# Wide attention's round: value products and projections behind the first two transposes, both key products behind the third

## What is computed

```python
xn = _layernorm(x, ln1_w, ln1_b)          # x here is the context, 77 tokens
latn = _layernorm(latents, ln2_w, ln2_b)  # the 128 tokens of the sequence
q = latn @ Wq
kv = concatenate([xn, latn], axis=1) @ Wkv
k, v = split(kv, 2, axis=-1)              # 205 keys, 16 heads of 64
weight = softmax(einsum('bhld,bhnd->bhln', q * scale, k * scale))
out = einsum('bhln,bhnd->bhld', weight, v).reshape(b, l, 1024)
return out @ Wo
```

## Time and profile before

| | us |
|---|---|
| median of 3 runs | 2099.02 |
| lowest and highest | 2098.89, 2105.73 |
| profiled execution | 2097.34 |
| its span | 2095.6 |

### The profile page before, as it was taken

The page is one execution under the profiler, slowest core; times in us unless marked ns, Lnnn a source line. Parts: engine busy times, 40 slices in busy tenths (PEclk is TensorE's granted clock), DMA queues, the critical chain, the costliest instruction groups (busy, mean ns, idle before and its releaser), DMA issues.

```text
span 2095.6 us, 45982 instructions
## 1 busy us (share of the span) xinstructions
PE 1925.5 (92%) x15235; PEld 1543.7 (74%) x15297; DVE 1463.9 (70%) x3292; ACT 1345.6 (64%) x3094; POOL 970.4 (46%) x1173
## 2 busy tenths in 40 slices
PE   6999999999999999974089999999899999999998
PEld 4877778888888888842078888887677777777776
DVE  5668667777666666657865676767787788677775
ACT  4676567777677677757745666787555555555554
POOL 3555543344344344300026555554366566556565
PEclk8999999999999999997589999999999999999999
DMA  6533300000000000000033434555233333333332
GB/s 182 170 116 110 94 2 2 2 2 2 2 2 2 2 2 2 2 1 1 0 99 99 120 103 109 155 165 160 69 117 122 122 121 124 114 119 122 121 128 91
DMA packets 139168, 161.12 MB, mean 77 GB/s; under 512 B 15340, under 2 KB 99244, under 8 KB 138796
## 3 DMA queue, kind: packets, MB, share of 16 engines
q1 hardware_dynamic: 132780, 153.46, 24.1%
q10 hardware_dynamic: 6160, 4.78, 0.7%
HBM read 119.75 MB, written 38.70 MB: 76 GB/s over the span
## 4 chain that ended last, share of the span: by engine, by line
PE 69%; issue 8%; POOL 8%; DVE 5%; ACT 5%; SPq 2%; DMA 2%; POOLq 0%; ACTq 0%; DVEq 0%
POOL h_lo L2245 7%; PE bank L993 6%; PE score_banks L273 6%; PE bank L1009 6%; PE score_banks L982 5%; PE bank L934 5%; PE bank L935 4%; PE bank L936 4%; PE bank L284 3%; PE score_banks L255 3%; PE score_banks L1902 3%; PE score_banks L1900 3%; PE score_banks L1901 3%; PE bank L1900 2%; PE score_banks L254 2%
## 5 line engine op out<-in xcount | busy, mean ns | idle before, releaser
L2245 POOL TENSOR_TENSOR h_lo<-h,h_hi 128x512 fp32r<-128x512 f32 x264 | 341.1, 1292 | 245.1 <-ACT h_hi L2026 245.0
L1432 POOL TENSOR_TENSOR pw<-ew,rw 128x410 f32<-128x410 f32 x256 | 222.5, 869 | 369.2 <-DVE rw L1282 369.2
L556 DVE TENSOR_REDUCE nmx<-score_banks 128x4 fp32r<-128x512 f32 (+1 forms) x384 | 237.4, 620 | 182.6 <-PE score_banks L255 179.3
L2019 ACT ACTIVATE sl<-score_banks 128x512 f32<-128x512 f32 x264 | 157.8, 598 | 240.1 <-PE score_banks L1902 237.6
L449 ACT ACTIVATE pt<-score_banks 128x512 f32<-128x512 f32 (+1 forms) x384 | 229.4, 599 | 119.8 <-PE score_banks L273 118.9
L2164 DVE TENSOR_TENSOR bank<-score_banks,sl 128x512 f32<-128x512 f32 x264 | 184.1, 697 | 144.2 <-PE score_banks L1902 114.3
L1146 ACT ACTIVATE ew<-score_banks,nmax 128x205 f32<-128x205 f32 x512 | 217.5, 434 | 103.1 <-DVE nmax L1275 101.9
L708 POOL TENSOR_SCALAR_AFFINE_SELECT pt<-pt 128x512 f32<-128x512 f32 x256 | 164.6, 643 | 177.2 <-ACT pt L449 177.2
L273 PE MATMUL score_banks<-q_pack,k_diag 128*128 128x128 f32 (+1 forms) x1536 | 236.8, 278 | 0.1
L273 PEld LDWEIGHTS score_banks<-q_pack,k_diag 128*128 128x128 f32 (+1 forms) x1536 | 188.4, 179 | 45.2 <-issue 36.4
L1900 PE MATMUL score_banks<-x_hi,w_hi 128*128 128x512 f32 x528 | 209.7, 397 | 0.1
(11 more groups left out here) (348 smaller groups left out, 4572.5 us busy)
## 6 DMA issues: line engine op xcount, KB each, us to landing
share_b<-share_rows SPq DMA_DIRECT2D x256, 256.0 KB, 3.1
q_rows<-q_hi SPq DMA_DIRECT2D x96, 128.0 KB, 2.8
q_pack<-q_rows SPq DMA_DIRECT2D x32, 384.0 KB
raw<-in_experts SPq DMA_DIRECT2D x33, 192.0 KB, 3.3
q_rows<-q_lo SPq DMA_DIRECT2D x48, 128.0 KB, 2.7
k_diag<-k_rows SPq DMA_DIRECT2D x64, 96.0 KB
q_pack<-q_rows SPq DMA_DIRECT2D x31, 192.0 KB
k_diag<-k_rows SPq DMA_DIRECT2D x124, 48.0 KB
```

What stands on the lines that cost most here:

```text
L556: nc.vector.tensor_reduce(m.nmx[:, b % 2, :, 0, c], m.score[c % 2][:, 0:HC * a.columns].rearrange("p (h k) -> p h k", h=HC)[:, :, 0:a.keys ...
L1432: nc.gpsimd.tensor_tensor(m.pw[:, n, :, :], m.ew[:, n % 2, :, :], m.rw[:, n % 2, :].unsqueeze(2).broadcast_to([128, 2, KW]), ALU.mult)\
L2245: nc.gpsimd.tensor_tensor(m.h_lo[:, k % 3, :], m.h[:, (k + u) % 2, :], m.h_hi[:, k % 3, :].bitcast(F32), ALU.subtract).then_inc(s.los, 1)
```

## The change

On TensorE the same operations are put in another order. Before, a round went: queries, value, T0, value, T1, half projection, key 2i+4, T2, key 2i+5, half projection, T3. Now it goes: queries, T0, value, half projection, T1, value, half projection, T2, key 2i+5, key 2i+4, T3. On VectorE the two value copies move behind one maximum each: the first copy now stands between maxima 2 and 3, the reciprocal of step 0 and maximum 2 come ahead of it. The semaphore `keyed`, which counted key products in order, becomes two, since the order of the two changes.

```diff
@@ class WideSemaphores
-        self.keyed = sem(f"{stage}_keyed")
+        self.first_keyed = sem(f"{stage}_first_keyed")
+        self.second_keyed = sem(f"{stage}_second_keyed")
@@ wide_tensor, key
-                 m.kvt_hi[:, v, :, 0:KP], m.kvt_lo[:, v, :, 0:KP]).then_inc(s.keyed, 1)
+                 m.kvt_hi[:, v, :, 0:KP], m.kvt_lo[:, v, :, 0:KP])\
+            .then_inc((s.first_keyed, s.second_keyed)[couple % 2], 1)
@@ wide_tensor, body
             queries(i + 2, m.mix)
+        transpose_probs(i, 0)
+        if ahead:
             pe.wait_ge(s.first_keys, i + 2)
...
             value(tile, m.ask)
-        transpose_probs(i, 0)
+        if i > 0:
+            project_out(i - 1, 0)
+        transpose_probs(i, 1)
         if ahead:
             pe.wait_ge(s.queries, i + 3)
             value(tile + 1, m.mix)
-        transpose_probs(i, 1)
         if i > 0:
-            project_out(i - 1, 0)
-        if ahead:
-            pe.wait_ge(s.values, tile + 1)
-            key(2 * i + 4, m.ask)
+            project_out(i - 1, 1)
         transpose_probs(i, 2)
         if ahead:
             pe.wait_ge(s.values, tile + 2)
             key(2 * i + 5, m.mix)
-        if i > 0:
-            project_out(i - 1, 1)
+            key(2 * i + 4, m.ask)
         transpose_probs(i, 3)
@@ wide_scalar, copy_keys
-        act.wait_ge(s.keyed, couple + 1)
+        act.wait_ge((s.first_keyed, s.second_keyed)[e], i + 1)
@@ wide_vector, copy_keys
-        dve.wait_ge(s.keyed, couple + 1)
+        dve.wait_ge(s.first_keyed, i + 1)
@@ wide_vector, body
             copy_queries(i + 2, m.mix)
-            copy_values(tile, m.ask)
         if ahead:
             reciprocals(i + 1, 0)
             maxima(i + 1, 2)
+        if more:
+            copy_values(tile, m.ask)
+        if ahead:
             maxima(i + 1, 3)
         if more:
             copy_values(tile + 1, m.mix)
```

More of the change, by code:

```diff
@@ L1129, in input_highs @@
         wait(act, s.valued, TILES * (p - 1))
-        wait(act, s.keyed, XC * (p - 1))
+        wait(act, s.first_keyed, QUADS * (p - 1))
+        wait(act, s.second_keyed, QUADS * (p - 1))
         wait(act, s.asked, QUADS * (p - 1))
```

## The result

| | before | after |
|---|---|---|
| median of the runs | 2102.38 us | 2123.0 us |
| lowest and highest | 2098.89, 2105.85 | 2118.34, 2129.04 |
| profiled execution | 2097.34 us | 2118.34 us |
| its span | 2095.6 us | 2116.6 us |
| first scores of the stage to the last | 624.2 us | 640.4 us |

The ratio is 1.0092, with a 95% interval of 1.0062 to 1.0121: slower by some 19 us, 13 to 25. The forecast was 2134.5, 35.5 more than before, in a range of 2112 to 2147. The sign and the mechanism held; the size was 1.8 times too large.

What follows compares the result with a forecast made beforehand. TensorE's order and its bank hand-overs were taken to bound each round. Longer rounds 15.5, the keys' copy 17.7 and VectorE's lateness 2.3 sum to 35.5 us: 2097.34 becomes 2132.8, plus 1.7 for the median, 2134.5; range 2112 to 2147.

Steps and rivals of the forecast that it cites:

- a round starts on VectorE's word: Round start on TensorE: the queries' weights load when VectorE has finished us_lo, plus 0.18 for the signal.
- Step 1: Behind T0, 0.70 earlier: ScalarE's copy waits for step 0's exponentials, starts at 586.09 instead of 586.47, gaining 0.38.
- the bound that I had priced at 6 us less: ScalarE's copy behind T0 may start 0.1 before the accumulator read ends; T1 comes 0.1 earlier, total 2128.
- Step 2: Ahead of T1 on TensorE: a stall of 0.18 for the bank's copy stays where 0.23 was.
- Steps 3 and 4: From T1 to behind T2: T2 is free, then the key product into mix waits for the second value copy, 0.33.
- The hidden-copy rival: Behind T2: the key product finds its bank free, T3 comes 0.07 earlier than before; +14, 2113 us; 10%.
- Step 5: Keys then T3, at 590.26 instead of 590.00: a round 0.25 longer, 15.5 us over 62 rounds.
- The first keys' copy: Behind T3, rounds g = 0 and 1: input or output transposes wait for bank ask, 0.59 in 30 rounds, 17.7 us.
- VectorE's lateness: Norm-step rounds of the first six pairs: keys' copy 1.42 later exceeds the slack to us_lo, 2.3 us over six rounds.
- no signal at all at 16 us less: Waits on VectorE: if its signal cost nothing, 0.18 less in 92 waits, total 2118.
- The faster one: Whole round: only hand-overs bound it, gaining 0.26, 2083 us, if T0's, value and first keys' copies come early enough; 3%.
- weights that are loaded ahead: TensorE's queue: by the skill's rule weights would be in the array before a stall ends, the sum some 9 lower.

Runs made afterwards that it cites:

- e2: The changed kernel with its two key products swapped (2i+4 into ask first) in rounds g = 0 and 1 alone; stage 622.2 us against 640.4.
- e6: The kernel before with the two waits of each transpose group swapped, the bank's first; stage 617.2 us against 624.2, ratio 0.9967.
- e5: The kernel before without TensorE's waits that an earlier wait covers, from the third round on; stage 623.5 us against 624.2, ratio 1.0032.

## Why the prediction was right, and where it was off

*No instruction is added or removed; the bound is the order.* Right: 45982 instructions before and after. But *a round starts on VectorE's word* was wrong: `us_lo` starts two rounds, not all, and from this the 0.18 was read.

*Step 1, the copy behind T0 is held by the exponentials.* Right in kind. T0 came 0.69 earlier (0.70 said). The copy starts 1.68 behind the queries' weights where I had 1.76: at 581.47, while the last accumulator read runs from 581.38 to 581.58. I had let it start only as that read ends. This is the bound that I had priced at 6 us less.

*Step 2, T1 still stalls.* 0.10, where 0.18 was said; the difference is the 0.08 of step 1.

*Steps 3 and 4, a new stall behind T2 for `vs`.* Right, in each of 62 rounds; 0.2 in size, not 0.33. The copy starts where I put it, the moment its product is there. The term that failed is the signal: 0.18 in the sum, 0.05 in the run. The hidden-copy rival (2113) is out by the 13.5 us of this wait on record.

*Step 5, a round is 0.25 longer.* It is 0.03. Key product and T3 add up as said (1.24 against 1.21); T3 stands 5.75 behind the queries' weights, where I had 5.93. A further 0.05 comes from what I hadn't costed: T3 no longer waits for the bank, its weights are loaded 0.19 ahead of its matmul, and the weighting starts 0.53 behind T3 instead of 0.58. Of 15.5 us, 1.6 were real.

*The first keys' copy, 0.59 in 30 rounds.* Right in place and count, 0.48 each in size (0.50 and 0.52 more a round, less the 0.03 of every round), so 14.4 for 17.7. Again it is the 0.13 of the signal. A slip of 0.02 went the other way: by the sum's own rows the weights were free to load at +0.36 (0.39 less 0.03), not at +0.38, so 0.61 less 0.13 is the 0.48. e2 shows the place of the two key products as the cause: with key 2i+4 first in those rounds alone, the stage loses 18.1 us, more than the whole change had added.

*VectorE's lateness, 2.3 us.* It didn't come at all: the rounds in question take 9.76 to 9.79 like their neighbours, and `us_lo` ends 0.16 to 0.17 ahead of the queries' weights as everywhere, or 0.05 in the round that was late before as well. From the start of the keys' copy to `us_lo` those rounds had 4.43 us (5.34 in the late one), and have 1.46 less, as the later copy demands. Idle time gave a part of that. The rest is that VectorE's work became shorter: the records of the norm steps sum to 0.8 to 1.4 us less in each of the twelve rounds (last section). The two late rounds didn't get later by it: the queries' weights came 2.54 and 2.37 behind the first scores before, 2.50 and 2.40 after.

By terms: 35.5, less 13.9 for the round, 3.3 for the keys' wait and 2.3 for VectorE, is 16.0; the stage shows 16.1. The 35.5 was too large mainly because one misread number, 0.13 too large, stood in 92 waits: 12.0 of the 19.5. Step 1's 0.08 in 62 rounds is 5.0 more, and VectorE 2.3; what is left is small and of both signs. The bound that I gave for it, no signal at all at 16 us less, was the right place to look, and I chose the middle without asking whether `us_lo` really released those weights. Another round, the late one at 434.88, would have told. The total, 2123.0, lies in the range but 1 us below the 2124 to 2147 that were the forecast's own part of it.

*Rivals.* The faster one named three conditions, and none came true: the copy behind T0 started too late, the value copy still takes 0.69, the keys' copy 0.58. As for weights that are loaded ahead, T3's in the changed kernel have nothing to wait for and load 0.19 ahead of their matmul, while in every waiting row shown here the weights load 0.05 to 0.11 behind the release (0.22 in e2). The Trainium skill says that weight loads are pulled ahead of matmuls in flight (TensorE: Matmul & The Clock Gate, "Step-by-step: what each phase is for"); the trace agrees for T3, and no weights were pulled ahead of a wait.

## What to carry to other kernels

Count a reordering by each shared bank: product, copy, next user. Work that is moved to cover one copy uncovers another, and here the copy that was uncovered stood in 30 of 64 rounds, in a branch of the code that the change doesn't touch. Before you price a hand-over from one gap, find a round in which the same release comes really late: only then does the gap measure the signal. And where several waits stand ahead of an instruction, write first the one that is released last; here that alone took 7 us off.

## What I hadn't expected of the hardware

**Which wait rides on the instruction.** Of the waits written ahead of a weight load, the trace has the first on the load itself and the further ones in semaphore instructions ahead of it on TensorE's queue, one or two waits in each, 0.05 long: the one for the bank stands at 587.10, just before T1's weights at 587.17. In e6 the load itself carries the bank's wait, and the separate one, for the probabilities, is over long before. Released by such an instruction, the weights load 0.11 behind the copy's end; released by the load's own wait, 0.05; and with one more separate wait behind the late one, 0.22 (e2). Waits that are long met cost next to nothing (0.02 a round for the 14 such instructions that e5 took out of each).

**Small VectorE operations that last as long as GpSimd's.** In the kernel before, a VectorE operation on 128x16 elements took 1.53 us while two of GpSimd's ran:

```profile
510.80 1.13 POOL L1453 TENSOR_TENSOR kv<-ca,affine 77x256 f32<-77x256 f32 x1
...
511.27 1.53 DVE L2461 TENSOR_TENSOR t<-r,t 128x16 f32<-128x16 f32 x1
...
511.90 0.86 POOL L1432 TENSOR_TENSOR pw<-ew,rw 128x410 f32<-128x410 f32 x1
```

In the changed kernel, where the keys' copy had pushed it behind GpSimd's work, the same operation took 0.16, though not every operation near it was shorter (the 128x768 one took 0.93 for 0.55), and `us_lo` of that round was on time:

```profile
516.21 0.16 DVE L2465 TENSOR_TENSOR t<-r,t 128x16 f32<-128x16 f32 x1
...
517.11 0.69 DVE L1289 TENSOR_TENSOR us_lo<-bank,us_hi 128x512 fp32r<-128x512 f32 x1
```

The record of 1.53 ends at 512.80, and GpSimd's second operation at 512.76. That they contend for the same port is my reading; I didn't test it.
